# Moving a batch's scaling and half of its transposed-block rounding from ScalarE to VectorE

## The reference

```
norm(x, t, gw, gb, bw, bb) = (t @ gw.T + gb) * x * rsqrt(mean(x*x, -1) + 1e-6) + (t @ bw.T + bb)
h  = norm(x, t, g1w, g1b, b1w, b1b)
y  = x + softmax_over_keys(q k^T / sqrt(32)) v @ Wo.T      # q, k, v = h @ Wq.T, Wk.T, Wv.T; 16 heads of 32
y2 = y + (silu(norm(y, g2..) @ gate_w.T) * (norm(y, g2..) @ hid_w.T)) @ out_w.T      # hidden size 2048
out = x + y2
```

## Time and profile before

| | |
|---|---|
| median of the runs | 2383.4 us (2380.82 to 2390.84) |
| span of the profiled execution | 2384.2 us, the only time shown for it |
| busy: PE, DVE, ACT, POOL | 96%, 70%, 54%, 60% of the span |
| mean granted clock of TensorE | 0.989 of full speed |
| batch 0 / 1 / 2 / 3 of attention, roughly | 374 / 329 / 330 / 333 us |
| feed-forward half | 1018 us |

### The profile page before, as it was taken

One profiled execution on the slowest core, in us unless ns is written; L12 is line 12 of the kernel. 1 busy time (PEld: TensorE's weight loads), 2 busy tenths in 40 slices (PEclk: granted clock), 3 DMA queues, 4 the chain that ended last, 5 costly groups with the idle time before them and its releaser, 6 DMA issues.

```text
span 2384.2 us, 38858 instructions
## 1 busy us (share of the span) xinstructions
PE 2279.8 (96%) x10848; PEld 1561.5 (65%) x10848; DVE 1658.1 (70%) x2719; ACT 1284.7 (54%) x2286; POOL 1421.4 (60%) x1331
## 2 busy tenths in 40 slices
PE   6899999999999999999999889999999999999998
PEld 5555447555457554465554468887888788888887
DVE  4777754677736777546777378877887788778877
ACT  3366672567762666735666654363436344544354
POOL 0299891699961898925999837504760466036701
PEclk9899999999999999999999999999999999999999
DMA  5321213222132222132221232046114621363125
GB/s 163 99 66 33 66 32 112 52 60 54 49 94 59 53 47 72 32 111 46 48 54 32 106 133 62 27 151 221 54 36 133 204 81 36 106 200 113 44 89 177
DMA packets 91333, 203.06 MB, mean 85 GB/s; under 512 B 15200, under 2 KB 15200, under 8 KB 89440
## 3 DMA queue, kind: packets, MB, share of 16 engines
q1 hardware_dynamic: 90672, 194.06, 27.4%
q10 hardware_dynamic: 432, 6.29, 0.7%
HBM read 130.03 MB, written 19.92 MB: 63 GB/s over the span
## 4 chain that ended last, share of the span: by engine, by line
PE 80%; DVE 6%; issue 5%; ACT 4%; DMA 2%; POOL 2%; SPq 2%; DVEq 0%; ACTq 0%; POOLq 0%
PE bank L1814 26%; PE bank L1828 12%; PE bank L927 10%; PE bank L1107 9%; PE bank L1046 8%; PE bank L1002 8%; PE bank L1033 3%; PE bank L1012 2%; POOL sums L500 1%; DVE pmax L754 1%; ACT probs L658 1%; SPq L365 1%; PE bank L988 1%; DMA wo_raw<-in_out_w 1%; DVE ow L1634 1%
## 5 line engine op out<-in xcount | busy, mean ns | idle before, releaser
L754 DVE TENSOR_REDUCE pmax<-bank 128x1 f32<-128x512 f32 x1024 | 651.9, 683 | 210.0 <-PE bank L1002 202.0
L658 ACT ACTIVATE probs<-bank 128x512 f32<-128x512 f32 x1024 | 566.2, 602 | 304.6 <-PE bank L1107 253.7
L500 POOL TENSOR_TENSOR sums<-sums,probs 128x512 f32<-128x512 f32 x432 | 540.7, 1287 | 0.0
L1107 PE MATMUL bank<-qs,ks 128*128 128x512 f32 x1024 | 435.6, 430 | 12.1 <-ACT probs L658 9.7
L1002 PE MATMUL bank<-ks,qs 96*128 96x512 f32 x1024 | 407.2, 410 | 30.0 <-DVE pmax L754 29.0
L1107 PEld LDWEIGHTS bank<-qs,ks 128*128 128x128 f32 x1024 | 192.7, 189 | 276.0 <-issue 130.7
L1828 PE MATMUL bank<-ow,aw 128*128 128x512 f32 x1536 | 360.8, 392 | 3.1 <-DVE ow L1634 3.0
L1814 PE MATMUL bank<-H_hi,wt_hi 128*128 128x512 f32 x896 | 350.6, 391 | 8.6 <-DVE H_lo L1669 8.3
L1814 PE MATMUL bank<-H_hi,wt_lo 128*128 128x512 f32 x896 | 350.1, 391 | 0.0
L1814 PE MATMUL bank<-H_lo,wt_hi 128*128 128x512 f32 x896 | 350.0, 391 | 0.0
L1828 PEld LDWEIGHTS bank<-ow,aw 128*128 128x128 f32 x1536 | 285.0, 188 | 65.7 <-issue 6.7
(11 more groups left out here) (181 smaller groups left out, 3321.4 us busy)
## 6 DMA issues: line engine op xcount, KB each, us to landing
raw<-in_gu_w SPq DMA_DIRECT2D x66, 512.0 KB, 3.6
wo_raw<-in_out_w SPq DMA_DIRECT2D x128, 256.0 KB, 2.8
qs<-qk_hi SPq DMA_DIRECT2D x256, 64.0 KB, 2.0
ks<-qk_hi SPq DMA_DIRECT2D x128, 128.0 KB, 2.4
x<-attn_out SPq DMA_DIRECT2D x10, 1024.0 KB, 8.5
x<-in_x SPq DMA_DIRECT2D x8, 1024.0 KB, 5.1
qs<-qk_lo SPq DMA_DIRECT2D x128, 64.0 KB, 2.0
ks<-qk_lo SPq DMA_DIRECT2D x64, 128.0 KB, 2.4
```

The costliest lines, as they stand in the source:

```text
L500: nc.gpsimd.tensor_tensor(total, first, probs[:, s % 2, h, :], ALU.add) \
L658: nc.scalar.activation(probs[:, s % 2, h, :], sbank[i % SB][:], ACT.Exp, scale=SCALE).then_inc(st_done, 1)
L754: nc.vector.reduce_max(pmax[:, t, h, hf:hf + 1], mbank[n % MB][:], AX_X).then_inc(sq_done, 1)
L1107: nc.tensor.matmul(sbank[i % SB][:], ks[:, g % 2, h, s * P:(s + 1) * P], qs[:, u % 3, h, :], start=True, stop=True).then_inc(st_ready, 1)
```

## The change

Three things, all in the loop over batches 0 to 2 (the last batch prepares nothing):

1. The four multiplications of x's second half with `inv` leave ACT (L538 at (6, 5, h)) and become DVE's (L728 at (6, 6, h), behind the last maxima).
2. For the four `("hT", k, 1)` tiles the affine step and the rounding leave ACT (L555, L559). DVE does the affine step as one `tensor_scalar` in the bank, then a `tensor_copy` into `hT_hi`, then the subtraction as before. Each waits for the one ahead of it through DVE's own semaphore (`link`).
3. PE, DVE and the counters no longer wait for or count ACT for these tiles (`act_reads`); at the first tile of the feed-forward half, one wait is added on `w_dve`.

The tiles of the lead and of the first half, `("hT", k, 0)`, stay as they were.

```diff
+def act_reads(tile, body=True):
+    return (tile[0], tile[-1]) != ("D", 1) and not (body and in_maxima_bank(tile))
...
-LINKS_PER_BATCH = NU * (2 + 2) + 1
+LINKS_PER_BATCH = NU * (2 + 2) + 1 + 2 * KT
...
-                        if (u, s) == (6, 5) and not last:
-                            scale_x(b, 1, h)
                         for tile in done_at(u, s, h, b):
-                            if tile[0] != "D":
+                            if tile[0] != "D" and act_reads(tile):
                                 work_tile(b, tile)
...
         def scale_x(b, hf, t):
-            n = hf
+            n = hf if b is None else b * 2 + 2 + hf
             dve.wait_ge(inv_ready, n + 1)
...
+                if body and in_maxima_bank(tile):
+                    link(nc.vector.tensor_scalar(bank[:], bank[:], cur_gain[:, k:k + 1], cur_bias[:, k:k + 1], ALU.mult, ALU.add))
+                    link(nc.vector.tensor_copy(hT[0][:, k, cols], bank[:]))
                 nc.vector.tensor_tensor(hT[1][:, k, cols], bank[:],
...
+                        if (u, s) == (6, 6) and not last:
+                            scale_x(b, 1, h)
...
         def evicted(b, tile):
-            pe.wait_ge(w_act, MISC_ACT(b, act_before(b, tile) + 1))
+            if act_reads(tile, b is not None):
+                pe.wait_ge(w_act, MISC_ACT(b, act_before(b, tile) + 1))
             pe.wait_ge(w_dve, MISC_DVE(b, dve_before(b, tile) + 1))
```

More of the change, by code:

```diff
@@ L141, in done_at, with in_maxima_bank @@
     return [m for m in (made_at(u, s, h), tile if part == KT - 1 else None, sums_at(u, s, h)) if in_batch(b, m)]
-def act_reads(tile):
-    return (tile[0], tile[-1]) != ("D", 1)
+def in_maxima_bank(tile):
+    return tile[0] == "hT" and tile[2] == 1
+def act_reads(tile, body=True):
+    return (tile[0], tile[-1]) != ("D", 1) and not (body and in_maxima_bank(tile))
 def dve_reads(tile):
@@ L155 @@
 MISC = Counter(len(LEAD_MISC), len(BODY_MISC))
-MISC_ACT = Counter(sum(map(act_reads, LEAD_MISC)), sum(map(act_reads, BODY_MISC)))
+MISC_ACT = Counter(sum(act_reads(m, False) for m in LEAD_MISC), sum(map(act_reads, BODY_MISC)))
 LEAD_DVE = [m for m in LEAD_MISC if dve_reads(m)]
@@ L207, in act_before @@
     order = order_of(b)
-    return sum(map(act_reads, order[:order.index(tile)]))
-def in_maxima_bank(tile):
-    return tile[0] == "hT" and tile[2] == 1
+    return sum(act_reads(m, b is not None) for m in order[:order.index(tile)])
 def wbank_before(b, tile):
@@ L557, in work_tile @@
                 n = hf * KT + k + 1
-                act.wait_ge(full, n if b is None else b * (NHALF * KT) + (NHALF * KT + n))
+                act.wait_ge(full, n if b is None else b * KT + (NHALF * KT + n))
                 nc.scalar.activation(hT[0][:, k, cols], bank[:], ACT.Copy).then_inc(w_act, 1)
@@ L733, in work_tile @@
             dve.wait_ge(w_ready, MISC(b, misc_index(b, tile) + 1))
-            if act_reads(tile):
+            if act_reads(tile, body):
                 dve.wait_ge(w_act, MISC_ACT(b, act_before(b, tile) + 1))
@@ L919, in vector_part @@
         batch(NB - 1)
-        assert Link.n == LINKS_PER_BATCH, Link.n
+        assert Link.n == LINKS_PER_BATCH - 2 * KT, Link.n
     def tensor_part(pe, lead):
@@ L1144, in attention_program @@
         "exps": [(st_done, SCORES_T(b, NT + NU * NS * GH) + SB)],
-        "affine": [(full, NB * (NHALF * KT))],
+        "affine": [(full, NHALF * KT + (NB - 1) * KT), (w_dve, MISC_DVE(b, 0))],
         "norm": [(x_scaled, NB * 8), (inv_ready, NB * 2)],
```

## The result

The changed kernel is slower: 2402.99 us (median of four runs, 2400.21 to 2405.55) beside 2382.11 us for the kernel before. The ratio is 1.009, with a 95% interval of 1.0076 to 1.0105. That is 21 us, where I forecast none. It lies at the place and has the size of the rival that I gave 4%.

What follows compares the result with a forecast made beforehand. PE is busy 96% of the span, but POOL's sums set the entry to unit 7 in batches 1 and 2. Terms of +0.72 - 0.77 = 0 gave 2383 us, likeliest 2381 to 2387, range 2376 to 2391.

Steps and rivals of the forecast that it cites:

- the rival that I gave 4%: Unit 6's end: POOL's gapless additions shut out DVE's scalings, PE waits 7.0 us more a batch at transposes; 2404; 4%.
- the price of the scaling: At (6, 6), four DVE scalings alternate with POOL's additions, each 0.18 us longer; 0.7 us lost, bounds 0 and 1.9.
- the sum: At `D` and the K projection behind it: +0.36 us each in batches 1 and 2, -0.8 in batch 0, together 0.
- A stretch of half clock can come or go as well: PE's clock at 1.2 GHz in place of 2.4, as in batch 0: costs at most 1.7 us, within the range.
- the stall for L743: Behind `D`, K's projection waits 0.34 us for DVE's subtraction; predicted to go, -0.34 us a batch.
- ACT's relief isn't the gain: 8.3 us a batch leave ACT, 25 us over three, but most lies beside POOL's gapless run.
- The rival in which the relief counts in full: Units 6 to 7: both of POOL's gaps waiting on ACT go in each batch, -6.3 us, 2377; chance 22%.
- The sum with POOL's loss at 0: Lower bound if scalings cost POOL nothing: -0.34 in batches 1 and 2 each, more in batch 0; -2.2 us in all.
- POOL sets `D`: Entry to unit 7, batches 1 and 2: PE's product waits for POOL's step 7 sums (1000.57, product 1000.71), however early ACT is.
- DVE's chain a tile: Second-half `hT` tiles: affine step 0.69 us (0.48 to 0.79), 2.15 us a tile on DVE, nearly the same latency as before.
- The ceiling: POOL's path from unit 6 to unit 7, step 5: all preparation costs 2.9 us a batch; gain under 8.6 us, 0.36%.

## Why the prediction was wrong

**The step that failed** is in the price of the scaling: "So they take turns: the DVE instruction waits for POOL's running one, and POOL's next is longer by 0.18", and with it "At (6, 6) POOL is in its gapless run, so every one of the four scalings meets it." The rows under it are right, but I carried them over from a place that differs in the one thing that counts. In the trace of before POOL's additions at 1510.50 and 1511.20 stood close behind a gap of 0.16 us, the wait of L1377 for L1392:

```profile
1509.81 0.74 POOL L1377 TENSOR_TENSOR s_ring<-raw 128x256 f32<-128x256 f32 x1 [0.16 <-POOL wt_lo L1392]
1510.50 0.74 POOL L1378 TENSOR_TENSOR s_ring<-raw 128x256 f32<-128x256 f32 x1
```

In the run at (6, 6) the last gap lies 19 us back. I had written down that POOL's run is gapless, and gave the case in which that matters 4%, "in each meeting seen DVE came next". All those meetings were near a gap, and no others were to be had: in the whole trace of before, no scaling, copy or two-input instruction of DVE within SBUF that was issued while POOL was busy came more than 6.5 us, or seven of POOL's instructions, behind the last gap. What the runs showed in place of turns is one wait of 10.8 us a batch for the first scaling and 0.47 us for each of the others, and with it 6.83 us in which PE stands at the transposes.

**Where the turns exist, the working holds up to `D`, and a term is missing behind it.** With one gap, the four scalings took 5.25 us from the first one's issue (predicted 995.2 - 989.94 = 5.26), and POOL's eight additions 10.53 us in place of 9.93, 0.6 more (predicted 0.7). `D` moved by 0.6 us. But the stretch from POOL's first addition of step 5 to that of the next unit took 35.3 us in each batch, 1.5 more than the 33.8 of batches 1 and 2 before, where the sum had 0.36. With ACT relieved, PE comes to `D` early and waits there for POOL, and its clock falls behind that wait. The product of `D` in batch 2, then the stretch at half clock (columns as in the section on the result):

```profile
1001.17 1.06 PE L1018 MATMUL bank<-sums,ones 128*32 128x512 f32 x8 [2.24 <-POOL sums L502]
```

```profile
1002.50:1005.90 3.40, 3.40 (x16) 2.03 (x9) 1.21 (x2) 0.89 (x2) 1.93 (x2) 0.50 0.04 10
```

With the gap earlier, at (6, 5, 1) or (6, 3, 1), the profiled executions show the same wait of 2.24 us; the half clock follows it in one batch of three, which takes 35.3 us, and not in the others, which take 33.6 to 33.8. The prediction had such stretches in its range ("A stretch of half clock can come or go as well"), not in its sum. The ratios of the kernels that take turns are 1.0005, 1.0018, 1.0019, 1.0022 and 1.0026, the last four clear of 1 by their intervals: 4 to 6 us, where the sum had said no change. Three stretches at half clock account for up to 4.5 us of that; the rest stays open.

**The rival's price was right.** Its +7.0 us a batch and 2404 compare with 6.83 us of waiting in batch 2 and 2403 us. That it comes so close is in part luck: the path of batch 2 grew by 6.3 us and not by 7.0. The sum left out the half clock behind the wait (0.75 us to `D`), and on the other side that PE now reached the transposes 0.56 us earlier in the run, without ACT's scalings ahead of the exponentials, and got back 0.7 us behind `D`, about half of it the stall for L743.

**ACT's relief isn't the gain: right.** With the scalings on ACT and 5.4 us less for it in unit 7 of a batch, the time is 0.9994 of before; with all 8.3 us gone from ACT and DVE's scaling off the contended form, 1.0004. The rival in which the relief counts in full (2377, a ratio of 0.9974) lies outside both intervals. A part of the relief does show on the path: from POOL's first addition of step 5 to that of the next unit the two kernels take 32.9 to 33.1 us in each batch, 0.7 to 0.8 less than before in batches 1 and 2 and 1.8 less in batch 0, some 3.3 us together. The sum with POOL's loss at 0 had 2.2. The times can't tell 3 us from nothing.

**POOL sets `D`: right.** With ACT relieved, POOL's gap of 1.18 us vanished and PE stood ready 1.25 us early, and `D` still came 0.14 us behind POOL's last sum.

**DVE's chain a tile.** The affine step from bank to bank takes 0.82 us, above even my upper end of 0.79; the tile takes 2.26 in place of 2.15. It stayed hidden, and the wait of L927 for the denominators' sum, 0.34 us on PE, is gone in the changed kernel, as predicted.

**The ceiling.** On the path to which it belongs the best version gained 0.8 us in batches 1 and 2, against 2.9. The ceiling wasn't tested by itself. No kernel here beats the one before by more than the measurement can tell.

## What to carry to other kernels

Before work is moved to VectorE beside a busy GpSimd, look at two things: whether the instruction contends with GpSimd at all (a scaling within SBUF and a two-input instruction did, reads from a bank and the accumulating form didn't), and whether GpSimd's additions have a gap shortly before. If they haven't, the price here wasn't a share of each instruction but the whole rest of GpSimd's run, and everything in order behind it. A wait on GpSimd's own last instruction, a gap of 0.08 us, was enough to end that; so was the accumulating form. A duration taken from elsewhere in a trace needs the same neighbours, not just the same instruction; here a form of 0.74 us that never waits was worth more than one of 0.47 that may wait for 10.8.

## What the runs showed of the hardware

- A DVE instruction that contends was shut out for 10.8 us, through nine additions of GpSimd that followed each other with no gap (issued during the first, ended behind the ninth), and for 11.9 us through one such and sixteen shorter ones. GpSimd's additions weren't made longer by it (9.85 us for eight, 9.93 before).
- A gap of about 0.08 us in GpSimd's run made the two alternate from then on (1.50 us for the scaling, 1.46 for the addition, beside 0.47 and 1.27 alone). The gap could lie 3 or 9 us ahead of the first DVE instruction. One of 0.23 us at 10.2 us worked in one batch of three. One of 0.16 us at 11.2, one of 0.08 at 15.1, and one of 0.68 at 19 in the changed kernel (at 14 with the scalings a step earlier) didn't, so a longer gap was no help at such distances. In GpSimd's instructions the edge is at about nine. The Trainium skill (SBUF — State Buffer, "SBUF: two separate sides") says that whichever starts first gets the shared pair for the whole instruction and the other fully blocks. The alternating runs fit that; the shut-out one goes beyond it, since a waiting instruction isn't next when the running one ends. Why the reach of a gap ends where it does stays open: no run here tells a count of instructions from a time.
- A `tensor_scalar` from bank to bank took 0.82 us, a copy from bank to SBUF 0.69, for the same 128x512 block.
- TensorE's wait of 6.8 us brought a stretch of 10.2 us at 1.2 GHz, of which 4.4 us lay behind the wait. A wait of 2.24 us was followed by 3.4 us at 1.2 GHz, in all three batches of one kernel and in one batch of three of two others.
